# A two-layer graph network on one core: the SBUF scratch for GpSimd's DMA descriptors at 8 KB a partition in place of 16 KB

## What is computed

```python
edge_index = jnp.stack([src, dst])
x = _layernorm(x + _L0_gnn_ref(x, src, dst, ...))
x = _layernorm(x + _L1_gnn_ref(x, edge_index, edge_attr_64, ...))
```

## Time and profile before

| | us |
|---|---|
| median of 3 runs | 16,960.74 |
| lowest and highest | 16,942.1 and 16,977.2 |
| the profiled execution | 16,936.29 |
| its span (first to last instruction) | 16,934.6 |
| busy: TensorE products, GpSimd, VectorE, ScalarE | 10,130.0, 9,610.4, 6,874.5, 3,232.9 |

### The profile page before, as it was taken

The page is one execution under the profiler, slowest core; times in us unless marked ns, Lnnn a source line. Parts: engine busy times, 40 slices in busy tenths (PEclk is TensorE's granted clock), DMA queues, the critical chain, the costliest instruction groups (busy, mean ns, idle before and its releaser), DMA issues. The chain is left out here.

```text
span 16934.6 us, 272856 instructions
## 1 busy us (share of the span) xinstructions
PE 10130.0 (60%) x65767; PEld 9071.1 (54%) x65768; DVE 6874.5 (41%) x21943; ACT 3232.9 (19%) x8136; POOL 9610.4 (57%) x10125
## 2 busy tenths in 40 slices
PE   3333334444455544544577777777777766777776
PEld 2233333444444444444566666557777766777775
DVE  5333333333333333333566666553333333333334
ACT  0000001111111111111000000143333333333333
POOL 4666665555555555555555555206666655666664
PEclk8555556777766777777777777787777777777777
DMA  6521212222222222222455555412222233222225
GB/s 222 189 47 47 48 47 65 81 83 83 85 83 83 84 84 83 85 82 82 123 149 148 147 147 149 93 53 64 64 64 64 64 67 68 64 64 64 64 64 75
DMA packets 2220524, 1490.56 MB, mean 88 GB/s; under 512 B 1358838, under 2 KB 2015382, under 8 KB 2218643
## 3 DMA queue, kind: packets, MB, share of 16 engines
q0 software_dynamic: 377360, 782.89, 16.7%
q1 hardware_dynamic: 1798712, 584.97, 15.3%
q10 hardware_dynamic: 44230, 120.70, 2.0%
HBM read 1115.52 MB, written 483.77 MB: 94 GB/s over the span
## 5 line engine op out<-in xcount | busy, mean ns | idle before, releaser
L1744 POOL DMA_INDIRECT p<-q_rows,small x3432 | 3240.0, 944 | 2770.3 <-DMA ring<-in_x,small 1013.4
L999 POOL DMA_INDIRECT edges_a<-ring,small x1664 | 1596.3, 959 | 1202.9 <-ACT ring L987 518.9
L999 POOL DMA_INDIRECT edges_b<-ring,small x1664 | 1596.1, 959 | 1113.6 <-issue 496.9
L894 DVE CUSTOM_DVE_ANT_0 ring<-bank,ring 128x99 f32<-128x99 f32 x3328 | 667.4, 257 | 3716.0 <-remote 3323.7
L752 POOL DMA_INDIRECT ring<-in_x,ring x1664 | 1569.8, 943 | 863.2 <-issue 486.4
L916 PE MATMUL bank<-ring,after 128*128 128x99 bf16 x3328 | 569.1, 261 | 2478.2 <-DVE small L894 2214.6
L1140 POOL DMA_INDIRECT ring<-in_x,small x1352 | 1275.3, 943 | 1009.6 <-PE bank L1172 526.6
L916 PEld LDWEIGHTS bank<-ring,after 128*128 128x128 bf16 x3328 | 373.9, 125 | 2618.6 <-DVE small L894 2326.2
L1160 PE MATMUL bank<-p,ring 128*128 128x129 f32 x8360 | 1393.0, 343 | 439.5 <-DVE ring L1088 276.9
L790 PE MATMUL bank<-ring 128*128 128x129 f32 x3328 | 846.8, 423 | 1338.3 <-DVE acc L711 709.6
L1160 PEld LDWEIGHTS bank<-p,ring 128*128 128x128 f32 x8360 | 1355.4, 257 | 500.0 <-issue 499.7
(11 more groups left out here) (277 smaller groups left out, 17185.9 us busy)
## 6 DMA issues: line engine op xcount, KB each, us to landing
p<-edges_b SPq DMA_DIRECT2D x530, 262.0 KB
p<-edges_a SPq DMA_DIRECT2D x520, 262.0 KB
ring<-bonds_by_dst SPq DMA_DIRECT2D x3344, 32.0 KB
bonds_by_dst<-in_bond ACTq DMA_DIRECT2D x5, 20625.0 KB
ring<-edges_b SPq DMA_DIRECT2D x1920, 33.0 KB
ring<-edges_a SPq DMA_DIRECT2D x1792, 33.0 KB
p<-q_rows,small POOLq DMA_INDIRECT x3432
ring<-in_x,ring POOLq DMA_INDIRECT x1664
```

The source lines that it names most:

```text
L999: pool.indirect_dma_start(out=c.edges[s], out_offset=bass.IndirectOffsetOnAxis(ap=pos[:, k:k + 1], axis=0), in_=rec[:, k, :], in_offset=No ...
L1744: pool.indirect_dma_start(out=gath[g][:, k, :], out_offset=None, in_=c.q_dram, in_offset=bass.IndirectOffsetOnAxis(ap=gidx[g][:, k:k + 1], ...
```

## The change

```diff
-    nc = _bacc.Bacc("TRN2", target_bir_lowering=False, num_devices=1)
+    nc = _bacc.Bacc("TRN2", target_bir_lowering=False, num_devices=1,
+                    dynamic_dma_scratch_size=8192)
```

## The result

| | before | after |
|---|---|---|
| median of 3 runs, us | 16,960.74 | 17,060.76 |
| lowest and highest, us | 16,942.1 and 16,977.2 | 17,044.2 and 17,078.9 |
| ratio, with its 95% interval | | 1.0055 [1.0033, 1.0077] |

The account below looks back on a forecast made before the run. No engine was full; loops through GpSimd's 10,115 indirect DMAs, about 1.25 us each, were taken to bound four stages. Terms of +0.8 us, nothing and nothing on 16,960.74 gave 16,961.5 us, range 16,905 to 17,018.

Parts of the forecast that it names:

- turn mark: A DMA 9 ns over the median where the scratch turns back to its start; forecast every 57th DMA instead of every 114th.
- part 1: All indirect DMAs: half the scratch turns twice as often, 89 more turns at 9 ns, +0.8 us (bounds nothing to 2 us).
- that rival: The scratch size doesn't reach the chip: mark stays at every 114th DMA, time at 16,960.7 us; chance 0.04.
- Part 3: Every tensor starts 8 KB a partition lower; priced at nothing, bounds 46 us either way.
- part 2: Fewer DMAs can stand open: 57 fill half the scratch, the kernel's own buffers hold 32 slots; priced at nothing.
- The first rival: Full scratch makes GpSimd wait for landings, 1.6 us more at each of 177 fillings: 283 us, 17,245 us; chance 0.08.
- The rule of the Trainium skill: Descriptor buffer can fill during writing, a smaller one sooner; counted against the change, but the sum stayed at +0.8 us.
- the four stages keep ... within some 10 us: Sign: the four stages that gather or scatter rows keep 2411, 5438, 2655 and 5457 us within some 10 us.

## Why the prediction was wrong

**Right.** The turn mark came at the 57th DMA, the 30th of L752, and 57 further on, as part 1 had it (line L752 in four stretches of the changed kernel, columns as in the earlier trace rows):

```profile
L752 POOL DMA_INDIRECT ring<-in_x,ring x29: 942/947/947, 220.4 to 255.4; - x29
...
L752 POOL DMA_INDIRECT ring<-in_x,ring x1: 957/957/957, 256.7 to 256.7; - x1
...
L752 POOL DMA_INDIRECT ring<-in_x,ring x56: 942/947/948, 258.0 to 339.1; - x56
...
L752 POOL DMA_INDIRECT ring<-in_x,ring x1: 957/957/957, 340.4 to 340.4; - x1
```

Ten ns over the median, 0.9 us in all. So the size reached the chip, and that rival falls. Part 3, the places, cost nothing, as priced.

**The step that failed is part 2**, "I price this at nothing", with "its cover is the gap between 32 and 57". I took it that entries come free when their DMA lands. By the runs GpSimd stops when the count is full, at 0.85 us every 32 gathers in `messages`; read as above, entries are cleared only then, many in one go, and GpSimd waits for what isn't hidden.

**The first rival was right in kind, and I threw it out by looking in the wrong place.** "The same would already happen every 114 DMAs, with GpSimd idle for 1.9 us": it does happen, with 1.86 us, ahead of the 114th gather of `messages`. I looked where the ring turns, 114 DMAs from the program's start; the count runs from each stage's start. Two things made its 283 us too high: most stops are hidden behind a group's earlier DMAs, and those of before have to be taken off. What it is worth is 48 us in `messages` by the sum above, and 37 by the means of three profiles of each size. That its 1.9 us met the measured 1.86 is luck: it was worked out from a landing, and the stops of 0.35 to 2.35 us with other sizes fit a time for each entry instead. The rule of the Trainium skill (Perfetto Trace Analysis, section "DMA Instruction — SWDGE (GPSIMD)") speaks of a descriptor buffer that can fill; it doesn't say that GpSimd stops. I wrote that the trace did not bear it out at today's size; the 35 stops in `messages` of the kernel before agree with it as far as a full count goes.

**What no step had** is the larger part, 92 us in the profiled run, and 50 by the means of three profiles of each size (5437, 5442 and 5477 us with 16 KB, 5469, 5507 and 5530 with 8). I treated a stop as a price to be added. In `sort_records` it is a push that shortens the stage, and the change took part of the push away: that stops do this is shown by those set by hand, and that the change's loss is this one is argued from the counts of broken rhythms, 31 of 38 stops and 18 of 42. The sentence "the four stages keep ... within some 10 us" held for two of four.

**What stays open.** Why about 31 entries stay uncleared in three stages, and 17 or 24 in `messages`; why 19 KB counts to 128; why 4 KB, where 28 fit, shows no stop, and yet stays slower than 16 KB when both have stops set by hand; and why TensorE's signal comes mostly only behind GpSimd's row of scatters. That a MEMSET of another length, or a wait, would break the rhythm as well wasn't tried.

## What to carry to other kernels

Before an edit to a buffer is priced at nothing because it is thought never to fill, look for the longest idle time inside groups that should be even, counted from the start of each stage, and not only at the place where the ring turns. Where a stage alternates between paces, list the pace group by group before summing prices: a small wait can be what keeps it quick, and then a change that removes waits makes it slower, and a stop set by hand pays (here 416 MEMSETs of 1.2 us, with 10 KB of scratch, gain 0.9% on the kernel before). The scratch's size isn't a knob that is better the larger it is, as 19 KB shows (1.0025): what counts is where in a group the stops fall.

## What the chip showed that I hadn't expected

- GpSimd stops for 0.35 to 2.5 us, at distances that the scratch's size sets; the lengths fit some 30 ns for each DMA since the last stop, and what a stop costs depends on its place in the group of DMAs.
- While GpSimd issues eight scatters without a break, VectorE and ScalarE idle 9.51 and 8.12 us on signals of TensorE whose products are recorded as done more than 7.7 us earlier; the signals' own updates are recorded that late, and SyncE's MOVEs take 0.69 us in place of 0.02.
- The kernel before took 16,937 to 16,952 us (medians) on three chips and 17,076 on a fourth, over 0.7% more; verdicts here rest on ratios of runs beside each other.
